# A graph network on one core: the attention stage's score rows made and broadcast three groups ahead, GpSimd's gathers without landing waits, SyncE's loads in eight parts

## What is computed

```python
h = (x @ W_lin + b_lin).reshape(N, 2, 64)
ee = (edge_attr @ W_edge + b_edge).reshape(-1, 2, 64)
x_i = h[src]; x_j = h[dst] + ee              # src, dst = edge_index
alpha = (x_i * att_i).sum(-1) + (x_j * att_j).sum(-1)
alpha = where(alpha >= 0, alpha, 0.2 * alpha)
amax = segment_max(alpha, src, N)
e = exp(alpha - amax[src])
alpha = e / (segment_sum(e, src, N)[src] + 1e-16)
out = segment_sum(x_j * alpha[:, :, None], src, N).mean(axis=1) + bias
```

## Time and profile before

| what | value |
|---|---|
| median of three runs | 15282.47 us (15275.27 to 15283.02) |
| the profiled execution | 15310.28 us, span 15308.5 us |
| granted TensorE clock, mean over the span | 0.705 of full speed |
| busy: PE, DVE, ACT, POOL | 62%, 47%, 25%, 61% |
| the two propagations, POOL's gathers | 7130.0 to 11941.9 us |
| the attention, POOL's gathers | 12070.8 to 15198.0 us, 1728 in number |

### The profile page before, as it was taken

The page is one execution under the profiler, slowest core; times in us unless marked ns, Lnnn a source line. Parts: engine busy times, 40 slices in busy tenths (PEclk is TensorE's granted clock), DMA queues, the critical chain, the costliest instruction groups (busy, mean ns, idle before and its releaser), DMA issues.

```text
span 15308.5 us, 194462 instructions
## 1 busy us (share of the span) xinstructions
PE 9559.4 (62%) x40895; PEld 6424.8 (42%) x40896; DVE 7227.6 (47%) x18628; ACT 3829.9 (25%) x8556; POOL 9352.3 (61%) x8465
## 2 busy tenths in 40 slices
PE   0366657766568887884666666666666455555554
PEld 0011112221123434333666664566666354554454
DVE  8876656776500000002333333333333477777775
ACT  0244454444111111111222222222222122222221
POOL 0278887888754454453777774577777355555553
PEclk9999999999878887885555555555555555555555
DMA  9922222222289998999444444344444444444444
GB/s 383 401 15 19 20 16 19 20 20 20 11 306 354 355 383 310 360 383 66 104 103 104 103 104 55 90 104 103 104 104 100 86 133 131 132 133 131 132 133 91
DMA packets 1579834, 2197.42 MB, mean 144 GB/s; under 512 B 979723, under 2 KB 1022795, under 8 KB 1551437
## 3 DMA queue, kind: packets, MB, share of 16 engines
q1 hardware_dynamic: 1004396, 1490.91, 32.3%
q0 software_dynamic: 453120, 343.50, 14.4%
q10 hardware_dynamic: 121698, 356.43, 6.3%
HBM read 1771.19 MB, written 419.98 MB: 143 GB/s over the span
## 4 chain that ended last, share of the span: by engine, by line
POOL 43%; DMA 21%; issue 19%; PE 10%; DVE 4%; SPq 1%; another core or an unknown queue 1%; ACT 1%; POOLq 0%; DVEq 0%; ACTq 0%
POOL gat L651 21%; POOL adj L619 12%; DMA arena<-adj 10%; POOL arena L651 9%; DMA arena<-h_table,ring_i 7%; PE bank L1035 6%; DMA adj<-put_n,put_at 4%; DVE arena L1362 1%; POOL rec_src L605 1%; PE same L1167 1%; PE same L1006 1%; DVE arena L1364 1%; DMA arena<-lo_row 0%; SPq L526 0%
## 5 line engine op out<-in xcount | busy, mean ns | idle before, releaser
L651 POOL DMA_INDIRECT gat<-q_table,ring_i x3456 | 3483.4, 1008 | 1533.7 <-issue 1051.6
L619 POOL DMA_INDIRECT adj<-put_n,put_at x1632 | 2558.7, 1568 | 1267.3 <-DVE put_at L1446 638.2
L651 POOL DMA_INDIRECT arena<-h_table,ring_i x1728 | 1699.5, 984 | 1556.6 <-DMA arena<-h_table,ring_i 948.2
L605 POOL DMA_INDIRECT rec_src<-pay,ring_i x1632 | 1607.1, 985 | 1488.3 <-ACTq L749 1005.9
L1189 PE MATMUL bank<-onehot_t,onehot 128*128 128x64 f32 x6912 | 1584.5, 424 | 1445.3 <-DVE acc L1584 934.9
L1189 PEld LDWEIGHTS bank<-onehot_t,onehot 128*128 128x128 f32 x6912 | 1507.0, 330 | 1521.8 <-DVE acc L1584 929.3
L1094 PE MATMUL same<-onehot 32*128 32x512 f16 x3264 | 1678.9, 615 | 621.1 <-DVE onehot L1417 391.8
L1035 PE MATMUL bank<-arena,hs 128*64 128x512 f32 x5880 | 1590.3, 704 | 587.9 <-DMA arena<-adj 586.5
L1179 PE MATMUL bank<-hs,arena 128*128 x6912 | 1564.9, 421 | 171.8 <-ACT arena L873 171.8
L1425 DVE TENSOR_SCALAR_CACHE_REDUCE onehot<-same 128x128 bf16<-128x128 f32 (+3 forms) x1632 | 1232.8, 755 | 842.6 <-PE same L1096 792.0
L1179 PEld LDWEIGHTS bank<-hs,arena 128*128 128x128 f32 x6912 | 1525.7, 333 | 174.1 <-issue 174.1
(11 more groups left out here) (277 smaller groups left out, 12721.0 us busy)
## 6 DMA issues: line engine op xcount, KB each, us to landing
arena<-adj SPq DMA_DIRECT2D x300, 2560.0 KB, 20.4
arena<-rec_src SPq DMA_DIRECT2D x3456, 69.0 KB
adj<-hs ACTq DMA_DIRECT2D x25, 6656.0 KB, 46.4
rec_src<-pay ACTq DMA_DIRECT2D x1, 119232.0 KB, 332.3
arena<-lo_row SPq DMA_DIRECT2D x3456, 32.0 KB
hs<-b_row SPq DMA_DIRECT2D x108, 1024.0 KB, 5.0
acc<-b_row SPq DMA_DIRECT2D x108, 1024.0 KB, 5.1
gat<-q_table,ring_i POOLq DMA_INDIRECT x3456
```

What stands on the lines that cost most here:

```text
L605: nc.gpsimd.indirect_dma_start(rec_src, bass.IndirectOffsetOnAxis(ring_i[:, q, u:u + 1], 0), pay[:, q, u, :], None, bounds_check=SLOTS - 1 ...
L619: nc.gpsimd.indirect_dma_start(counts, bass.IndirectOffsetOnAxis(put_at[:, b // 3 % 4, c:c + 1], 0), put_n[:, b // 3 % 4, c:c + 1], None, ...
L651: nc.gpsimd.indirect_dma_start(rows[n][:, u, :], None, table, bass.IndirectOffsetOnAxis(ring_i[:, n, u:u + 1], 0)).then_inc(landed[n], 16)
```

## The change

It makes the score rows (`edge_scores`, transpose, copy, store, broadcast) of group n+3 instead of n+2 in body n, on DVE, PE, ACT and SP. It takes the landing wait out of POOL's `gathers`. SP's record load covers two groups in every second body (groups n+6 and n+7), and the record, position and broadcast loads are each issued as eight DMAs of 16 partitions (`parts_of`), with the semaphore values raised to match.

```diff
--- before.py
+++ after.py
@@ -170,6 +170,7 @@
         aend += 2 * U * P
         wrow = [arena[:, aend + n * U * LA:aend + (n + 1) * U * LA].rearrange("p (u h w) -> p u h w", u=U, h=HEADS) for n in range(2)]
         aend += 2 * U * LA
+        rec_flat = arena[:, aend:aend + 8 * U * 10].rearrange("p (t r) -> p t r", r=10)
         rec8 = [arena[:, aend + n * U * 10:aend + (n + 1) * U * 10].rearrange("p (u r) -> p u r", u=U) for n in range(8)]
         aend += 8 * U * 10
         ai_tab = arena[:, aend:aend + NH * HEADS]
@@ -383,7 +384,7 @@
         v_pen = sem("v_pen")
         d_pen = sem("d_pen")
         t_gat = [sem(f"t_gat{n}") for n in range(8)]
-        t_rec = [sem(f"t_rec{n}") for n in range(8)]
+        t_rec = [sem(f"t_rec{n}") for n in range(4)]
         t_lo = [sem(f"t_lo{n}") for n in range(4)]
         t_bb = [sem(f"t_bb{n}") for n in range(2)]
         d_bst = sem("d_bst")
@@ -548,22 +549,28 @@
             sp.dma_start(nodes_rows(h_table), proj[:, :, 0:HW]).then_inc(d_table, 16)
             sp.dma_start(pen10, pen_row.to_broadcast([P, NG * 10])).then_inc(d_pen, 16)
 
+            def parts_of(load, landed):
+                for q in range(SPLIT):
+                    load(slice(q * SLICE, (q + 1) * SLICE)).then_inc(landed, 16)
+
             def scores(i, n):
-                if live(i, n + 7):
+                if n % 2 == 0 and live(i, n + 6):
+                    at = (n + 6) % 8
                     hold(sp, t_w, nth(i, n - 1))
-                    sp.dma_start(rec8[(n + 7) % 8], rec[:, bass.ds(i * (8 * U) + (n + 7) * U, U), 0:10])\
-                        .then_inc(t_rec[(n + 7) % 8], 16)
+                    parts_of(lambda ps: sp.dma_start(rec_flat[ps, at * U:(at + 2) * U, :],
+                                                     rec[ps, bass.ds(i * (8 * U) + (n + 6) * U, 2 * U), 0:10]), t_rec[at // 2])
                 if live(i, n + 3):
                     hold(sp, t_m, nth(i, n - 1))
                     hold(sp, t_rel, nth(i, n - 1))
-                    sp.dma_start(lo_l3[(n + 3) % 4], lo_rows[bass.ds(i * 8 + (n + 3), 1), :].to_broadcast([P, U * P]))\
-                        .then_inc(t_lo[(n + 3) % 4], 16)
-                if live(i, n + 2):
-                    hold(sp, t_cb, nth(i, n + 2))
-                    sp.dma_start(b_row[n % 4].rearrange("(j e) -> j e", e=P), b_sb[n % 2]).then_inc(d_bst, 16)
-                    hold(sp, d_bst, nth(i, n + 2) * 16)
-                    hold(sp, t_m, nth(i, n))
-                    sp.dma_start(b_bc[n % 2], b_row[n % 4:n % 4 + 1].to_broadcast([P, 2 * U * P])).then_inc(t_bb[n % 2], 16)
+                    parts_of(lambda ps: sp.dma_start(lo_l3[(n + 3) % 4][ps],
+                                                     lo_rows[bass.ds(i * 8 + (n + 3), 1), :].to_broadcast([SLICE, U * P])), t_lo[(n + 3) % 4])
+                    hold(sp, t_cb, nth(i, n + 3))
+                    r = (n + 1) % 4
+                    sp.dma_start(b_row[r].rearrange("(j e) -> j e", e=P), b_sb[(n + 1) % 2]).then_inc(d_bst, 16)
+                    hold(sp, d_bst, nth(i, n + 3) * 16)
+                    hold(sp, t_m, nth(i, n + 1))
+                    parts_of(lambda ps: sp.dma_start(b_bc[(n + 1) % 2][ps],
+                                                     b_row[r:r + 1].to_broadcast([SLICE, 2 * U * P])), t_bb[(n + 1) % 2])
 
             eights(sp, scores)
             sp.wait_ge(v_h, 7)
@@ -643,10 +650,8 @@
                 pool.wait_ge(d_scat[q], EI * 16 * U)
 
 
-            def gathers(table, rows, landed, i, n, before, free):
-
-                if not free:
-                    hold(pool, landed[(n - 1) % len(landed)], i * (16 * U) + before)
+            def gathers(table, rows, landed, n):
+
                 for u in range(U):
                     nc.gpsimd.indirect_dma_start(
                         rows[n][:, u, :], None, table,
@@ -654,7 +659,7 @@
 
             def node_rows(k, i, n):
                 hold(pool, l_idx, i * 4 + (k * NG + n + 1))
-                gathers(q_table[k], gat4, l_gat, i, n, 0, True)
+                gathers(q_table[k], gat4, l_gat, n)
 
             for k in range(2):
                 pool.wait_ge(d_table, 16 * (1 + k))
@@ -664,13 +669,13 @@
                     for n in range(4):
                         node_rows(k, i, n)
 
-            def score_rows(i, n, first=False):
+            def score_rows(i, n):
                 hold(pool, t_idx, nth(i, n))
-                gathers(h_table, gat8, t_gat, i, n, (n > 0) * 16 * U, first)
+                gathers(h_table, gat8, t_gat, n)
 
             pool.wait_ge(d_table, 16 * 3)
             for n in range(8):
-                score_rows(0, n, first=n == 0)
+                score_rows(0, n)
             with pool.Fori(1, NG // 8) as i:
                 for n in range(8):
                     score_rows(i, n)
@@ -912,10 +917,11 @@
                 if live(i, n):
                     act.wait_ge(t_s, nth(i, n))
                     act.activation(score[n % 4], score[n % 4], ACT.Exp).then_inc(t_ex, 1)
+                if live(i, n + 3):
+                    act.wait_ge(t_bt, nth(i, n + 3))
+                    act.wait_ge(d_bst, nth(i, n + 1) * 16)
+                    act.copy(b_sb[(n + 1) % 2], bank[(n + 1) % 2][0:2 * U, 0:P]).then_inc(t_cb, 1)
                 if live(i, n + 2):
-                    act.wait_ge(t_bt, nth(i, n + 2))
-                    act.wait_ge(d_bst, nth(i, n) * 16)
-                    act.copy(b_sb[n % 2], bank[n % 2][0:2 * U, 0:P]).then_inc(t_cb, 1)
                     his = buckets(act, 1, i, n + 2, 8)
                     for b in range(PAIRS):
                         last = act.copy(nt[(n + 2) % 4][:, 0:2, b + 1], ai_tab[:, bass.ds(his[b] * HEADS, HEADS)])
@@ -924,7 +930,7 @@
                     act.wait_ge(t_mm, nth(i, n))
                     act.activation(oht_l3[n % 2], lo_l3[(n + 2) % 4], ACT.Relu, bias=1.0, scale=-1.0).then_inc(t_rel, 1)
                 if live(i, n + 3):
-                    done = i * 32 + ((n + 3) // 4 * 16 + 16)
+                    done = i * (32 * SPLIT) + ((n + 3) // 4 + 1) * 16 * SPLIT
                     act.wait_ge(t_lo[(n + 3) % 4], done)
                     act.activation(lo_l3[(n + 3) % 4], lo_l3[(n + 3) % 4], ACT.Abs, bias=neg_p[:, 0:1]).then_inc(t_abs, 1)
 
@@ -1233,10 +1239,10 @@
                     tr=TR_ATT, chunk=transposes(TR_ATT, 5))
 
             def scores(i, n):
-                if live(i, n + 2):
-                    pe.wait_ge(t_b, nth(i, n + 2))
-                    pe.wait_ge(t_cb, nth(i, n))
-                    nc.tensor.transpose(bank[n % 2][0:2 * U, 0:P], b_e[(n + 2) % 4], ident[:]).then_inc(t_bt, 1)
+                if live(i, n + 3):
+                    pe.wait_ge(t_b, nth(i, n + 3))
+                    pe.wait_ge(t_cb, nth(i, n + 1))
+                    nc.tensor.transpose(bank[(n + 1) % 2][0:2 * U, 0:P], b_e[(n + 3) % 4], ident[:]).then_inc(t_bt, 1)
                 if live(i, n + 1):
                     pe.wait_ge(t_nt, nth(i, n + 1))
                     pe.wait_ge(t_rel, nth(i, n + 1))
@@ -1656,7 +1662,7 @@
 
             def edge_scores(i, n):
                 dve.wait_ge(t_gat[n % 8], i * (16 * U) + (n // 8 * 16 * U + 16 * U))
-                dve.wait_ge(t_rec[n % 8], i * 16 + (n // 8 * 16 + 16))
+                dve.wait_ge(t_rec[n % 8 // 2], i * (16 * SPLIT) + (n // 8 + 1) * 16 * SPLIT)
                 v.tensor_tensor(by_edge(b_e[n % 4]), gat8[n % 8][:, :, HEADS * D:HW], rec8[n % 8][:, :, S5:S5 + HEADS],
                                 ALU.add).then_inc(t_b, 1)
 
@@ -1681,7 +1687,7 @@
                                 seen(n)[:, :, 2:4], ALU.subtract).then_inc(t_s, 1)
 
             def mask_scores(i, n):
-                dve.wait_ge(t_bb[n % 2], i * 64 + (n // 2 * 16 + 16))
+                dve.wait_ge(t_bb[n % 2], i * (64 * SPLIT) + (n // 2 + 1) * 16 * SPLIT)
                 dve.wait_ge(t_abs, nth(i, n))
                 for b in range(PAIRS):
                     e = slice(b * 2 * P, (b + 1) * 2 * P)
@@ -1761,8 +1767,8 @@
 
                 if n < 0 and isinstance(i, int) and i == 0:
                     index(i, n + 8)
-                if live(i, n + 2):
-                    edge_scores(i, n + 2)
+                if live(i, n + 3):
+                    edge_scores(i, n + 3)
                 if now:
                     alpha_sum(i, n)
                 else:
```

## The result

The changed kernel takes **15463.7 us** (median of three, 15460.4 to 15483.7) against 15282.5 before: a ratio of 1.0126, interval 1.011 to 1.0141. It is slower by 181 us, where a gain of 561 was predicted. The first rows are the stage's busy time by window; the columns are those of the earlier trace rows.

What follows compares the result with a forecast made beforehand. SP's issuing was to replace POOL's landing wait as the bound: (14.37 − 11.65) × 207.5 = −564, opening +3, padding 0, so −561 us from 15282.5 to 14721, range 14450 to 14990.

Steps and rivals of the forecast that it cites:

- The landing wait, and what bounds then: Attention stage: POOL's 4.3 us landing wait sets the 14.37 us pace; without it DVE needs 10.61 us per group, POOL 10.51.
- rival A: SP's parts cost less or its waits overlap, so DVE or POOL bounds at 10.6 to 10.8 us: 14520, chance 0.24.
- The lead: Score rows one group earlier: costed at 0, some 9 us of cover; without it broadcasts reach DVE's masks 1.5 us late.
- SP's parts: SP's queue: 21 DMAs in an even group instead of 4, mean 11.65 us per group, making SP the bound.
- store until broadcast: SP's time from storing the score row to issuing its broadcast, mostly the store's landing wait: 1.8 us per group.
- slack of 3.3 us: ACT's position (lo) rows: SP may lag 3.3 us before ACT's next Exp is late, enough to average even and odd groups.
- POOL busy over 65%: Sign expected in the profile after: POOL busy over 65% in the attention stage, its landing waits gone.
- The padding end: Last 8.5 groups, index always row 0: taken at 18.4 us per group as now, so 0; bounds -57 and +218 us.
- The opening: Start of the stage: DVE waits for four gathered groups, not three, +10 us less three 2.3 us landing waits: +3.
- D: Slower: SP's parts go out slower beside POOL's unbroken stream, mean pitch from 0.58 us; +290 us, 15570, chance 0.07.
- B: SP bounds at 12.5 us per group and the padding end sticks at 44 us a group: 15115, chance 0.08.
- C: DVE still waits for the same landings because the gathers' queue can't deliver faster: 15280, chance 0.05.

Runs made afterwards that it cites:

- experiment 1: Changed kernel with the broadcast load as one DMA of 128 partitions, records and positions still in eight parts: 14502.6 us, ratio 0.949.
- experiment 5: Kernel before with only POOL's landing wait taken out, whole loads, score rows two groups ahead: 14914.2 us, ratio 0.9749.
- experiment 4: Changed kernel with the broadcast in four parts of 32 neighbouring partitions: 14793.2 us, ratio 0.9684.
- experiment 3: Changed kernel with the broadcast in four parts of 32 partitions taken in steps of four: 14620.8 us, ratio 0.9572.
- experiment 8: Changed kernel with the broadcast in eight parts of 16 partitions, each taking every eighth partition: 15183.4 us, ratio 0.9934.
- experiment 9: Changed kernel with the record load alone as one DMA of 128 partitions, positions and broadcast in eight parts: 15352.6 us, ratio 1.0041.
- experiment 10: Changed kernel with the position load alone as one DMA of 128 partitions, records and broadcast in eight parts: 15111.8 us, ratio 0.9882.
- experiment 7: Changed kernel with POOL's landing wait put back, all loads still in eight parts: 15679.2 us, ratio 1.0245.
- experiment 11: Experiment 1's kernel with empty record slots' index set to their partition's number instead of 0: 14412.6 us, ratio 0.9426.
- experiment 2: Changed kernel with records, positions and broadcast each as one DMA of 128 partitions: 14557.4 us, ratio 0.9527.
- experiment 6: Changed kernel with all loads whole and POOL's landing wait put back, leaving only lead and paired records: 15250.5 us, ratio 0.9967.
- experiment 12: Experiment 2's kernel with empty record slots' index set to their partition's number instead of 0: 14437.9 us, ratio 0.9446.

## Why the prediction was wrong

**The landing wait, and what bounds then: right.** DVE's 10.61 us showed as 10.6 in experiment 1; rival A's 14520 is that kernel's 14503.

**The lead: right.** The masks' wait is in experiment 5 where it was put. The pace was 12.5 instead of 12.1.

**SP's parts: the step that failed.** It said "8 for lo rows, 8 for the broadcast, 1 store", priced the issues, and took "store until broadcast 1.8". The sum was 11.65 us per group; measured are 15.24. Mean distances between SP's runs from 12500 to 14000 us, per group:

| term | predicted | measured |
|---|---|---|
| records (half of each pair's) | 2.2 | 2.4 |
| positions | 3.7 | 4.0 |
| store until broadcast | 1.8 | 4.0 |
| broadcast run and next gap | 3.7 | 4.0 |
| further waits | 0.25 | in the gaps |
| a gap of 7 us once per round of the loop | none | 0.85 |

The issue prices held to within 10%. The term that is wrong is "store until broadcast": 2.2 us of the missing 3.6. The rest is 0.85 for the gap and some 0.3 on each of the other runs. The prediction counted what a part costs SP and not what it costs the DMA engines; it took the engines' 0.46 for slack.

Experiments 1, 4 and the change show that the queue needs 4.9, 7.4 and 9.9 us of every engine per group with the broadcast whole, in four parts of neighbours and in eight, and experiments 3 and 8 that strided parts avoid this (5.0 and 5.5). The wait for the store follows: it has the same queue, and it is the store with no record load between it and the last broadcast that waits long (5.8 us on the mean, against 2.2). With the engines this full even the issue prices would not have held for fewer parts (experiments 9 and 10).

The model for the parts, propagation, never split a load of 8 KB per partition; its split loads have 4.4 and 2 KB. Experiment 10 shows that a load of 2 KB pays almost nothing of the excess; the one of 4.4 KB no run has whole. Where SP then falls behind, ACT stands at the position rows, which is the queueing that the prediction named; its slack of 3.3 us was used up. Of the signs that it gave, POOL busy over 65% failed (53%), and the mean part pitch above 0.58 us that was to mark a slower kernel did not come, though the kernel is slower.

**The gap of 7 us** stands in no row of before. It comes once per eight groups, between the broadcast of an odd group and the next record load:

```profile
14043.07 4.15 SPq L572 DMA_DIRECT2D hs<-b_row  x8
14052.73 3.87 SPq L560 DMA_DIRECT2D arena<-rec_src  x8
```

4.15 us of broadcast from 14043.07, then nothing until 14052.73: 5.5 us here, 7.1 on the mean of 12. The kernels of experiments 1, 7, 8 and 11 have it too (5.7, 7.9, 3.5 and 5.7 us on the mean); those of experiments 2 to 6, 9, 10 and 12 don't have it at that place. SP waited for nothing that the profile shows. It is not SP's alone: in the kernel before, TensorE's weight loads have such a gap of up to 7.0 us about once per round, 23 times in 2500 us ("issue": the engine waited for nothing that the profile shows):

```profile
PEld bank L1245 <- issue: 159.7, 23, 7.0
```

That speaks for something at the loop's return, but what it is stays open; no experiment is on it alone. In experiment 8 it is worth 0.4 us of the pace, in the change 0.85.

**The padding end: right on the net.** It was costed as before. The two profiled executions differ by 150 us and not by 181, since that of the kernel before lies 28 us above its median. By DVE's reductions groups 20 to 200 cost 156 us more (15.24 against 14.38 us each), those ahead of them 11 more, and from group 200 to the last it is 247 us against 248. There the slow groups stayed (17.5 to 19.2 us) and the last five went faster (12 to 14), which cancels the slower normal groups: the sum is right, its parts are not. What slows those groups, the one row that every padding slot names, is shown by experiments 11 and 12.

**The opening: +3 predicted.** From POOL's first gather to DVE's first reduction it is 34.9 us against 26.0, so +9. But the stage itself begins 25 us earlier in the profiled execution after, which no step of the prediction and no experiment explains. Together: 156 + 11 - 1 + 9 - 25 = 150.

**Rivals.** A would have come from the same change with one load left whole. D had the right sign, but by another mechanism: its threshold was a mean part pitch of 0.58 us, and the measured one is 10.4 / 20 = 0.52. B and C are out: the pace is above B's 12.5 and the padding end did not stick at B's 44 us a group, and DVE no longer waits for gathers. What D's mechanism says does show in experiments 9 and 10, where a run of eight is held up to 5.9 and 8.3 us, but there the broadcast's parts hold it up and not POOL's stream: with the broadcast whole and POOL as free (experiment 1) the position run is 3.8 us.

The Trainium skill's rule cited in the prediction ("DMA: Bandwidth & Descriptors", Rules for kernel authors: one 128-partition transfer rather than disjoint ranges) was the better guide than the rows of another stage: for the broadcast it is worth 961 us. For records and positions it is slightly wrong here (whole is 55 us slower in experiments 1 and 2, and 25 in 11 and 12, which is within the noise).

## What to carry over

Price a split transfer twice: what it costs the queue that issues it, and what it costs the DMA engines, whose share of the stage must be read before and after against the bytes. By these runs a load of 8 KB per partition is best left over all 128 partitions in one DMA, and when it must be split, every n-th partition taken for a part. A price taken from another stage need not hold for a larger transfer, nor beside fuller engines; and a wait on a DMA's landing inside an issuing loop puts into the pace whatever occupies the queue ahead of it.

## What I had not expected of the hardware

- 1024 KB to 128 partitions: 4.9 us of each DMA engine per group (everything in the queue) as one DMA, 7.4 in parts of 32 neighbours, 9.9 in parts of 16 neighbours, but 5.0 and 5.5 in strided parts of 32 and 16.
- Loads of 2 KB per partition in parts of 16 neighbours add almost nothing to that (9.9 us split, 9.8 whole; with the record load 4.9 split, 4.3 whole).
- With the broadcast in such parts SP's issues are held up: eight position issues took 8.3 us instead of 3.9 when the record parts ahead of them were gone.
- A DMA with stepped partitions costs SP 0.66 us per issue and not 0.47.
- Gathers of 128 rows that all read one row of 256 bytes held the DMA engines at 0.88; spread over 128 rows, 0.43 at the same rate of gathers.
